# Two transformer blocks on one core: four staging tiles for weights, a new order of the opening, and GpSimd's long operations in pieces

## The chip, the cores and the metric

The kernel runs on one core of one Trainium2 chip. The metric is the device time of one execution in microseconds (us). The core has four compute engines that run beside each other: TensorE (PE in the profile; its weight loads are PEld), VectorE (DVE), ScalarE (ACT) and GpSimd (POOL). SyncE (SP) issues DMA transfers. Each engine takes its own instructions strictly in order, and engines wait for each other by semaphores.

## The reference

```python
x  = L0_attn_qkv                                     # (8, 256, 256)
xn = layernorm(x)
x  = x + attn0(xn) + ffn0(xn)                        # block 0
xn = layernorm(x)
x  = x + attn1(xn) + ffn1(xn)                        # block 1
```

`attn0` is causal attention with 16 heads of 16 channels and ALiBi slopes, with probabilities kept at or above 1e-10. `ffn0` has 8 experts, `silu(x @ Wg[e]) * (x @ Wu[e]) @ Wd[e]`, summed with weights that a small router makes from a sigmoid, a window and the two best. `attn1` is plain causal attention with its own weights. `ffn1` has two ternary layers: each weight becomes alpha * sign(W) where |W| is over 0.05 of the largest |W|, and alpha is the mean of those |W|; between them stands a gelu, and the result is quantized to 4 bits with one scale for the whole tensor.

## The kernel before, in words

The batch has 8 items of 256 tokens. The kernel makes one pass per item. Pass 0 (`"first"`) does block 0 of item 0 and the whole preparation of the weights; six passes of a loop (`"steady"`) and one more (`"last"`) do block 1 of one item beside block 0 of the next; `"final"` does block 1 of the last item and the quantization. So the list has nine parts, and only `"first"` loads and prepares weights.

The order of the work is written out by hand, as words in `ORDER_TEXT`, one text for each engine and kind of pass. A word names a step (`gate`, `score`, `split`) and its argument (`gate:2`: expert 2). Steps of one name run in the order of their arguments, whatever order the words have (`in_turn`). SyncE has no text of its own and follows TensorE's. An engine does for each word what its own `do` has under that name, or nothing.

The steps that matter here:

- `ln0a`, `ln0b`: layer norm of block 0 (VectorE; GpSimd makes `rstd` at L850). In pass 0 GpSimd then issues its own loads (`load_weights`, L818) and adds the bias `ob` (L844), and for that it waits for both `ob` loads.
- `split:i`: one of 14 weight tiles of 1024 columns, turned from float32 into a high and a low float16 part. SyncE loads it into a staging tile (`load_raw`, L674), ScalarE writes the high part (L965), and VectorE the low part (L1337). For splits 3, 5, 7, 9, 11 and 13 (`POOL_SPLITS`) ScalarE also writes a scaled copy (L967) and GpSimd makes the low part (L869). `SPLIT` lists them: 0 is the qk weights of block 0, 1, 3, 4, 6 ... are gate and up weights of experts 0, 1, 2, 3 ..., and 2, 5, 8, 11 are down weights of two experts each. There are two staging tiles, which borrow the room of `v_sb[1]` and `yx_sb`; the load of split i waits until the low part of split i - 2 is done.
- `vsplit`: the same for the v weights.
- `tr0`: transposes of the normed x (PE L1109), with high and low parts `xt_hi` (ACT L978) and `xt_lo` (DVE L1402). `xe` is GpSimd's copy of these for the experts (L875).
- `q0`, `k0` (PE L1135, ACT L995 and L998) and `l0` (DVE L1407): queries and keys with their parts. At `l0` SyncE stores them to DRAM (`store_parts`, L689) and reads them back in another layout (`load_stack`, L700).
- `v0`: values and the router's logits. `rt1`, `rt2`: the router.
- `setup:1` (GpSimd, L855 to L865): the four bias tables of the scores, from the slopes.
- `score` (PE L1223, DVE L1555, ACT L1037), `norm` (DVE L1580), `turn` (PE L1233, ACT L1046), `value`: attention of block 0.
- `gate`, `up`, `down`: an expert. At `up` VectorE writes `hid0` (L1502), ScalarE its high part `h_hi` (L1018) and GpSimd its low part `h_lo` (L880); `down` on TensorE (L1173) waits for that low part. `h1` is the same in block 1 (L903).
- `tern:i`, `tmx`, `tsm`: the two ternary weight matrices, 2048 columns each. VectorE finds the largest and the signs (L1345, L1352, L1355), GpSimd multiplies (L918), ScalarE sums (L958, L960), TensorE turns the sums (L1119), and VectorE makes alpha (L1370). TensorE starts the loop only when both are done.

GpSimd's text for pass 0 begins `ln0a xe split:3 setup:1 split:5 up`. The change does not touch it.

## Time and profile before

| | us |
|---|---|
| median of 3 runs | 765.38 (764.9 to 766.98) |
| profiled execution | 762.38 |
| its span, first to last instruction | 760.6 |

| engine | busy us | share |
|---|---|---|
| TensorE | 644.9 | 85% |
| VectorE | 570.8 | 75% |
| ScalarE | 465.4 | 61% |
| GpSimd | 270.1 | 36% |

The mean granted clock of TensorE was 0.958 of its full 2.4 GHz. All times below are us from the start of the span. A row of the timeline has its start, its duration, the engine, the line, the operation, output and inputs with their shapes (partitions x columns), a count, and in brackets how long the engine had been idle before it and what ended that. TensorE's matmuls overlap, so the distance between starts tells more than a duration. An engine with the letter q behind its name is the engine's instruction queue, which issues DMAs.

### The profile page before, as it was taken

The numbers are of one execution on the slowest core, as the hardware profiler recorded it, in microseconds if no ns is written. First come the engines' busy times: TensorE is split into PE (matmuls) and PEld (weight loads), VectorE is DVE, ScalarE is ACT, GpSimd is POOL, SyncE is SP. The second block draws the span as 40 slices with busy tenths as digits, with TensorE's granted clock in tenths as the row PEclk, the third lists the DMA queues.
The fourth block names the chain that finished last, engine by engine and source line by source line (L and its number), as shares of the span: only waits on it lengthen the run. The fifth ranks groups of instructions, "written<-read, shape, count | busy, mean of one in ns | idle before, by whom it ended". The sixth has DMA issues, their size and how long they took to land.

```text
span 760.6 us, 19948 instructions
## 1 busy us (share of the span) xinstructions
PE 644.9 (85%) x6455; PEld 480.6 (63%) x6455; DVE 570.8 (75%) x2203; ACT 465.4 (61%) x1223; POOL 270.1 (36%) x386
## 2 busy tenths in 40 slices
PE   1476676989989997999889997999899997999773
PEld 0354554767666775777666775777676775767542
DVE  4489867796687948796779858796779768886557
ACT  2567765954379454965389445965398435963652
POOL 7846541224404241142404241233313331135336
PEclk9989998999999999999999999999999998999996
DMA  6843021300303030302212030302211030300453
GB/s 203 273 127 117 8 77 49 97 17 16 124 14 110 14 110 28 109 1 69 83 35 76 14 110 28 110 4 68 80 58 53 14 110 16 112 3 1 153 181 110
DMA packets 49555, 56.72 MB, mean 75 GB/s; under 512 B 5104, under 2 KB 40048, under 8 KB 49520
## 3 DMA queue, kind: packets, MB, share of 16 engines
q1 hardware_dynamic: 46480, 52.44, 21.6%
q0 software_dynamic: 1056, 2.62, 1.0%
q10 hardware_dynamic: 1984, 1.21, 0.5%
q8 instruction: 19, 0.31, 0.2%
q14 instruction: 16, 0.13, 0.1%
HBM read 33.71 MB, written 22.54 MB: 74 GB/s over the span
## 4 chain that ended last, share of the span: by engine, by line
PE 58%; DVE 16%; ACT 11%; issue 8%; POOL 2%; DMA 2%; ACTq 1%; SPq 1%; DVEq 1%; POOLq 0%
PE gen_ps L1162 16%; PE gen_ps L1173 9%; PE gen_ps L1135 6%; PE value_ps L1280 5%; PE gen_ps L1193 4%; PE gen_ps L1210 3%; ACT hid L1025 3%; PE value_ps L1286 3%; PE score_ps L1223 2%; ACT probs L1037 2%; DVE probs L1555 2%; DVE inv L1591 2%; DVE probs L1580 2%; PE turn_ps L1249 2%; PE turn_ps L1233 2%
## 5 line engine op out<-in xcount | busy, mean ns | idle before, releaser
L880 POOL TENSOR_TENSOR h_lo<-hid,h_hi 128x512 f16<-128x512 f32 x64 | 74.4, 1163 | 271.6 <-ACT h_hi L1018 271.6
L1037 ACT ACTIVATE probs<-probs,nmax 128x256 f32<-128x256 f32 (+1 forms) x256 | 113.4, 446 | 29.0 <-DVE nmax L1555 28.6
L1162 PE MATMUL gen_ps<-xe_hi,gu_hi 128*128 128x256 f16 x512 | 101.0, 280 | 2.1 <-issue 2.1
L1162 PE MATMUL gen_ps<-xe_lo,gu_hi 128*128 128x256 f16 x512 | 100.6, 279 | 0.0
L1162 PE MATMUL gen_ps<-xe_hi,gu_lo 128*128 128x256 f16 x512 | 100.4, 279 | 0.0
L1555 DVE CUSTOM_DVE_ANT_0 probs<-score_ps,bias 128x256 f32<-128x256 f32 (+1 forms) x256 | 79.1, 351 | 16.5 <-PE score_ps L1225 16.5
L1065 ACT ACTIVATE et<-turn_ps 128x384 f32<-128x384 f32 x124 | 54.0, 489 | 50.9 <-PE turn_ps L1255 48.6
L1569 DVE CUSTOM_DVE_ANT_0 junk<-score_ps,bias 128x256 bf16<-128x256 f32 x248 | 73.6, 353 | 14.2 <-PE score_ps L1225 13.3
L1580 DVE TENSOR_SCALAR probs<-probs,rsum 128x256 f32<-128x256 f32 (+1 forms) x256 | 76.5, 341 | 4.6
L1014 ACT ACTIVATE tanh_sb<-gen_ps 128x512 f32<-128x512 f32 x64 | 37.8, 591 | 64.6 <-PE gen_ps L1162 64.5
L889 POOL TENSOR_SCALAR_AFFINE_SELECT et<-et 128x256 f32<-128x256 f32 x128 | 51.3, 423 | 73.0 <-ACT et L1065 73.0
L1223 PE MATMUL score_ps<-k_stack,q_stack 64*128 64x256 f16 x252 | 36.3, 285 | 44.0 <-DVE nmax L1555 26.0
L1046 ACT ACTIVATE pt<-turn_ps 128x384 f32<-128x384 f32 x128 | 60.4, 482 | 20.3 <-PE turn_ps L1235 20.2
L1173 PE MATMUL gen_ps<-wd_hi,h_hi 128*128 128x256 f16 x256 | 50.1, 278 | 9.7 <-issue 6.8
L1223 PEld LDWEIGHTS score_ps<-k_stack,q_stack 64*128 64x128 f16 x252 | 12.2, 93 | 72.2 <-DVE nmax L1555 30.7
L1162 PEld LDWEIGHTS gen_ps<-xe_hi,gu_hi 128*128 128x128 f16 x512 | 47.7, 100 | 14.3 <-issue 8.4
L1162 PEld LDWEIGHTS gen_ps<-xe_lo,gu_hi 128*128 128x128 f16 x512 | 51.3, 100 | 7.0
L1513 DVE SCALAR_TENSOR_TENSOR acc<-gen_ps,w,acc 128x256 f32<-128x256 f32 x112 | 48.8, 477 | 9.2 <-PE gen_ps L1173 9.2
L1162 PEld LDWEIGHTS gen_ps<-xe_hi,gu_lo 128*128 128x128 f16 x512 | 51.2, 100 | 6.9
L1502 DVE SCALAR_TENSOR_TENSOR hid<-gated,gen_ps 128x512 f32<-128x512 f32 x64 | 43.8, 684 | 11.4 <-PE gen_ps L1162 10.7
L903 POOL TENSOR_TENSOR h_parts<-hid,h_parts 128x512 f16<-128x512 f32 x32 | 37.3, 1178 | 38.4 <-ACT h_parts L1032 38.4
L1497 DVE SCALAR_TENSOR_TENSOR gated<-tanh_sb,gen_ps 128x512 f32<-128x512 f32 x64 | 43.6, 682 | 9.7 <-ACT tanh_sb L1014 9.7
(225 smaller groups left out, 1662.7 us busy)
## 6 DMA issues: line engine op xcount, KB each, us to landing
scr_q<-parts SPq DMA_DIRECT2D x32, 256.0 KB, 2.7
scr_k<-parts SPq DMA_DIRECT2D x32, 256.0 KB, 3.0
q_stack<-scr_q SPq DMA_DIRECT2D x64, 128.0 KB, 3.0
k_stack<-scr_k SPq DMA_DIRECT2D x64, 128.0 KB, 3.1
x<-in_x SPq DMA_DIRECT2D x8, 256.0 KB, 2.7
y_dram<-yx_sb SPq DMA_DIRECT2D x7, 256.0 KB, 2.2
x_dram<-yx_sb SPq DMA_DIRECT2D x7, 256.0 KB, 2.2
out_dram<-gu_hi SPq DMA_DIRECT2D x7, 256.0 KB, 2.2
```

The costliest lines, as they stand in the source:

```text
L880: pool.tensor_tensor(h0_lo[:, e], hid0[:, e], h0_hi[:, e], ALU.subtract).then_inc(s_h0l, 1)
L889: pool.affine_select(out=on_diagonal, in_=on_diagonal, compare_op=ALU.is_ge, fill=0.0, base=0, pattern=[[0, NT], [1, P]], channel_multipli ...
L1037: last = act.activation(probs[:, k, lo:hi], probs[:, k, lo:hi], ACT.Exp, scale=-1.0, bias=nmax[:, k, j:j + 1], accum_out=esum[:, k, j:j + 1])
L1046: act.activation(pt[:, slot:slot + 3].rearrange("p t q -> p (t q)"), turn_ps[s % 2][:, 0:3 * P], ACT.Copy).then_inc(s_ev[0], 1)
L1065: act.activation(et[:, s % TURNED], pair_of(st)[hp][:, 0:3 * P], ACT.Exp).then_inc(s_ev[1], 1)
L1162: last = pe.matmul(g[:, S * f:S * f + S], w[:, st.arg, m, k, cols], xx[:, k, :], start=(i == 0), stop=(i == len(terms) - 1))
L1173: last = pe.matmul(g[:, D * t:D * t + D], h[:, st.arg % 2, f, P * t:P * t + P], w[:, st.arg, f, :], start=(i == 0), stop=(i == len(terms) ...
L1223: pe.matmul(pair[hp][:, 0:S], q[rows[hp], i, P:S], k[rows[hp], i, :], start=True, stop=True)
L1513: dve.scalar_tensor_tensor(acc[:, t], g[:, D * t:D * t + D], w8[:, t, e:e + 1], (xb[0] if st.place == 0 else acc)[:, t], ALU.mult, ALU.add)\
L1555: last = dve.tensor_tensor_reduce(out=probs[:, k, lo:hi], in0=g[:, lo:hi], in1=bias0[:, s, blo:S], scale=-1.0, scalar=BIG, op0=ALU.add, op ...
L1569: last = dve.tensor_tensor_reduce(out=junk[:, hp, lo:hi], in0=pair_of(st)[hp][:, lo:hi], in1=bias1[:, blo:S], scale=-1.0, scalar=BIG, op0= ...
L1580: last = dve.tensor_scalar(probs[:, k, lo:hi], probs[:, k, lo:hi], rsum[:, k, j:j + 1], CLAMP, ALU.mult, ALU.max)
```

## The change

It has four parts.

1. Four staging tiles instead of two (`RAW = 4`). The new two take the room of the q and k stacks of block 1, which are now one tensor. The load of split i waits for the low part of split i - 4.
2. The small loads move. ScalarE issued fourteen loads ahead of its work; now it issues four (`bqk0`, `temp`, `vb0`, `wv0`), which have a semaphore of their own, `s_c0`. SyncE issues the others behind its first weight tiles. `setup:2` on VectorE needs only the first group; what belongs to block 1 is the new step `setup:3`.
3. A new order of pass 0's opening on TensorE, ScalarE and VectorE. `q0` and `k0` follow `tr0` at once, on TensorE and on ScalarE, and VectorE's `l0` comes ahead of `split:1`. VectorE's memset (`setup`) comes ahead of its wait for x. ScalarE's `split:1`, `split:2` and `split:3` stand behind `k0`.
4. GpSimd's long operations in pieces of 256 columns: the low part of a split in four, `h_lo` and `h1` in two, the ternary product in eight. The semaphore is raised by the last piece.

```diff
+RAW = 4
 "tensor": "first":
-            ln0a ln0b setup split xe split:1 setup:2 vsplit tr0 split:2 split:3 l0 q0 v0 split:5 k0 gate
-            setup:1 rt1 v0:1 norm:1 up gate:1 score norm split:4 rt2 score:1 up:1 split:6 down score:2
+            ln0a ln0b setup split xe split:1 setup:2 setup:3 vsplit tr0 q0 k0 l0 split:2 split:3 v0 split:5
+            gate setup:1 rt1 v0:1 norm:1 up gate:1 score norm split:4 rt2 score:1 up:1 split:6 down score:2
 "scalar": "first":
-            split:1 split vsplit tr0 split:2 q0 split:3 k0 gate v0 v0:1 split:5 split:4 gate:1 up score rt2
+            split tr0 vsplit q0 k0 split:1 split:2 split:3 gate v0 v0:1 split:5 split:4 gate:1 up score rt2
 "vector": "first":
-            ln0a split setup ln0b split:1 vsplit tr0 setup:2 split:2 v0 l0 gate rt1 v0:1 up split:4 gate:1
+            setup ln0a split ln0b setup:2 tr0 vsplit l0 split:1 v0 split:2 gate rt1 setup:3 v0:1 up split:4
+            gate:1 score score:1 up:1 norm rt2 norm:2 split:6 score:2 down gate:2 score:3 norm:1 score:4
...
+        stack1 = sb("stack1", [2 * KR, 2, 2, H // 4, S], F16)
+        q_stack.append([stack1[:, u, 0] for u in range(2)])
+        k_stack.append([stack1[:, u, 1] for u in range(2)])
...
+        raw += [stack1[:, u].rearrange("p a h n -> p (a h n)").bitcast(F32) for u in range(2)]
...
             def load_raw(i):
-                if i >= 2:
-                    sp.wait_ge(*lo_done(i - 2))
-                dst, (what, a) = raw[i % 2], SPLIT[i]
+                if i >= RAW:
+                    sp.wait_ge(*lo_done(i - RAW))
+                dst, (what, a) = raw[i % RAW], SPLIT[i]
...
-                if name == "split" and st.arg + 2 < len(SPLIT):
-                    load_raw(st.arg + 2)
+                if name == "split" and st.arg + RAW < len(SPLIT):
+                    load_raw(st.arg + RAW)
...
             load_x(Index(None, 0))
             load_raw(0)
             load_raw(1)
+            sp.dma_start(slope_sb[:], slopes.partition_broadcast(P)).then_inc(s_c, 16)
+            load_raw(2)
+            load_raw(3)
+            sp.dma_start(ob[0][:], ob0.partition_broadcast(P)).then_inc(s_ob, 16)
...
+            sp.dma_start(ob[1][:], ob1.partition_broadcast(P)).then_inc(s_ob, 16)
...
-                    pool.tensor_tensor(lo, raw[st.arg % 2], hi, ALU.subtract).then_inc(s_lop, 1)
+                    for c in range(0, 2 * NK * D, D):
+                        last = pool.tensor_tensor(lo[:, c:c + D], raw[st.arg % RAW][:, c:c + D], hi[:, c:c + D], ALU.subtract)
+                    last.then_inc(s_lop, 1)
...
-                    pool.tensor_tensor(h0_lo[:, e], hid0[:, e], h0_hi[:, e], ALU.subtract).then_inc(s_h0l, 1)
+                    for f in range(NF):
+                        last = pool.tensor_tensor(h0_lo[:, e, f], hid0[:, e, f], h0_hi[:, e, f], ALU.subtract)
+                    last.then_inc(s_h0l, 1)
...
-                        pool.tensor_tensor(tern_of(i)[0], tern_of(i)[0], tern_of(i)[1], ALU.mult).then_inc(s_tu, 1)
+                        w, t = tern_of(i)
+                        for c in range(0, NK * HID, D):
+                            last = pool.tensor_tensor(w[:, c:c + D], w[:, c:c + D], t[:, c:c + D], ALU.mult)
+                        last.then_inc(s_tu, 1)
...
         def _(act):
+            act.dma_start(bqk[0][:], bqk0).then_inc(s_c0, 16)
+            act.dma_start(half_t[:], temp.partition_broadcast(P)).then_inc(s_c0, 16)
+            act.dma_start(vb[0][:], vb0.partition_broadcast(P)).then_inc(s_c0, 16)
+            act.dma_start(wv_raw[0].rearrange("p (k n) -> p k n", k=NK), wv0.rearrange("(k p) n -> p k n", p=P)).then_inc(s_wv[0], 16)
```

## Rows read from the trace of the kernel before

**Rows 1.** The chain of waits in one steady pass, 375 to 460 us, by line.
```profile
by line: PE gen_ps L1162 17.2%; PE gen_ps L1173 9.7%; PE gen_ps L1135 8.3%; issue 6.9%; PE value_ps L1280 6.1%; PE gen_ps L1210 4.4%; PE gen_ps L1193 4.2%; ACT probs L1037 4.0%; ACT hid L1025 3.6%; PE value_ps L1286 3.1%; PE score_ps L1223 
```
**Rows 2.** Busy time by stretch: stretch, length, engines, clock, DMA; steady pass, then pass 0.
```profile
205.00:292.00 87.00, 80.98 (x824) 61.03 (x823) 66.52 (x273) 53.83 (x148) 25.80 (x41) 0.98 0.18 57
...
52.00:105.00 53.00, 39.48 (x345) 30.46 (x343) 48.88 (x139) 39.44 (x95) 23.20 (x22) 0.94 0.18 55
```
**Rows 3.** Timeline of the opening, all engines, 0 to 24 us.
```profile
1.31 0.46 SPq L679 DMA_DIRECT2D v_sb<-in_wqk  x1
...
10.73 1.06 ACT L965 ACTIVATE qk_hi<-v_sb 128x1024 f16<-128x1024 f32 x1
...
13.23 1.02 DVE L1317 MEMSET v_sb<- 128x1152 f32 x1 [0.19 <-issue]
...
20.32 0.84 ACT L995 ACTIVATE rest<-gen_ps,bqk 128x256 f32<-128x256 f32 x2 [0.53 <-PE gen_ps L1135]
...
21.29 0.38 PE L1135 MATMUL gen_ps<-xt_hi,qk_hi 128*128 128x256 f16 x2
...
21.73 1.04 ACT L965 ACTIVATE gu_hi<-yx_sb 128x1024 f16<-128x1024 f32 x1
...
22.67 1.04 ACT L967 ACTIVATE yx_sb<-yx_sb 128x1024 f32<-128x1024 f32 x1
...
23.79 2.12 POOL L869 TENSOR_TENSOR gu_lo<-yx_sb,gu_hi 128x1024 f16<-128x1024 f32 x1 [2.35 <-ACT yx_sb L967]
```
**Rows 4.** Timeline of GpSimd, 26 to 42 us.
```profile
26.41 2.75 POOL L861 TENSOR_TENSOR bias<-at,slope_sb 128x1024 f32<-128x1024 f32 x1
...
33.40 1.89 POOL L861 TENSOR_TENSOR bias<-at,slope_sb 128x1024 f32<-128x1024 f32 x1
...
38.69 2.13 POOL L869 TENSOR_TENSOR wd_lo<-yx_sb,wd_hi 128x1024 f16<-128x1024 f32 x1
40.77 1.15 POOL L880 TENSOR_TENSOR h_lo<-hid,h_hi 128x512 f16<-128x512 f32 x1
```
**Rows 5.** Timeline of TensorE: the first score and the first two `down` steps.
```profile
37.80 0.40 PE L1223 MATMUL score_ps<-k_stack,q_stack 64*128 64x256 f16 x2 [7.92 <-DMA k_stack<-scr_k]
...
42.02 0.38 PE L1173 MATMUL gen_ps<-wd_hi,h_hi 128*128 128x256 f16 x2 [1.05 <-issue]
...
48.89 0.58 PE L1173 MATMUL gen_ps<-wd_hi,h_hi 128*128 128x256 f16 x2 [3.34 <-issue]
```
**Rows 6.** Timeline of SyncE: the first store of q and k.
```profile
27.43 0.37 SPq L694 DMA_DIRECT2D scr_q<-parts  x1
```
**Rows 7.** Timeline: the two ternary products on GpSimd, and VectorE behind the first.
```profile
78.52 4.08 POOL L918 TENSOR_TENSOR hid<-hid,t_sb 128x2048 f32<-128x2048 f32 x1 [4.09 <-DVE t_sb L1355]
...
87.44 0.42 DVE L1370 TENSOR_REDUCE t_tot<-gen_ps 128x2 f32<-128x256 f32 x1 [1.34 <-PE gen_ps L1119]
...
104.79 5.10 POOL L918 TENSOR_TENSOR h_parts<-h_parts,t_sb 128x2048 f32<-128x2048 f32 x1 [8.98 <-DVE t_sb L1355]
```
**Rows 8.** DMA issues, 0 to 20 us: count, KB each, median us to landing.
```profile
v_sb<-in_wqk SPq DMA_DIRECT2D x1, 512.0 KB, 7.7
...
x<-in_x SPq DMA_DIRECT2D x1, 256.0 KB, 5.5
```
**Rows 9.** Chain of waits, 0 to 150 us: start, us; twelve matmuls at either clock.
```profile
17.50 2.73 PE gen_ps L1135 x12
...
93.17 1.31 PE gen_ps L1173 x12
```
**Rows 10.** Timeline of ScalarE: the high part of expert 1's `hid0`.
```profile
46.77 0.62 ACT L1018 ACTIVATE h_hi<-hid 128x512 f16<-128x512 f32 x1
```
**Rows 11.** Groups of GpSimd by shape: busy us, mean ns.
```profile
L844 POOL TENSOR_TENSOR xb<-acc,ob_sb 128x256 f32<-128x256 f32 x16 | 11.2, 723 | 39.8 <-DVE yx_sb L1543 36.8 <-DVEq L1617 2.9
```
**Rows 12.** Timeline, 146.5 to 149 us: VectorE beside GpSimd.
```profile
146.93 1.45 DVE L1580 TENSOR_SCALAR probs<-probs,rsum 128x256 f32<-128x256 f32 x2
...
147.10 1.20 POOL L903 TENSOR_TENSOR h_parts<-hid,h_parts 128x512 f16<-128x512 f32 x1 [2.94 <-ACT h_parts L1032]
```

More of the change, by code:

```diff
@@ L155 @@
         "first": """
-            ln0a split setup ln0b split:1 vsplit tr0 setup:2 split:2 v0 l0 gate rt1 v0:1 up split:4 gate:1
-            score score:1 up:1 norm rt2 norm:2 split:6 score:2 down gate:2 score:3 norm:1 score:4 down:1
-            norm:3 up:2 split:8 gate:3 score:5 norm:4 up:3 tern score:6 norm:5 tmx tern:1 gate:4 score:7
-            down:2 split:10 score:8 norm:6 norm:7 down:3 score:9 up:4 norm:8 score:11 score:10 norm:9
-            score:12 norm:11 tern:2 gate:5 down:4 score:13 +ln0a up:5 norm:10 norm:12 split:12 tsm tern:5
-            tern:6 score:14 gate:6 norm:13 up:6 +ln0b score:15 gate:7 down:5 tmx:1 norm:15 vsplit:1 norm:14
-            +tr0 up:7 down:6 tern:8 tern:7 +l0 +v0 +v0:1 op0 down:7 tsm:1 tern:11
+            setup ln0a split ln0b setup:2 tr0 vsplit l0 split:1 v0 split:2 gate rt1 setup:3 v0:1 up split:4
+            gate:1 score score:1 up:1 norm rt2 norm:2 split:6 score:2 down gate:2 score:3 norm:1 score:4
+            down:1 norm:3 up:2 split:8 gate:3 score:5 norm:4 up:3 tern score:6 norm:5 tmx tern:1 gate:4
+            score:7 down:2 split:10 score:8 norm:6 norm:7 down:3 score:9 up:4 norm:8 score:11 score:10
+            norm:9 score:12 norm:11 tern:2 gate:5 down:4 score:13 +ln0a up:5 norm:10 norm:12 split:12 tsm
+            tern:5 tern:6 score:14 gate:6 norm:13 up:6 +ln0b score:15 gate:7 down:5 tmx:1 norm:15 vsplit:1
+            norm:14 +tr0 up:7 down:6 tern:8 tern:7 +l0 +v0 +v0:1 op0 down:7 tsm:1 tern:11
         """,
@@ L501, in two_blocks @@
         s_x = sem("s_x")
+        s_c0 = sem("s_c0")
         s_c = sem("s_c")
@@ L508, in two_blocks @@
         s_w1 = sem("s_w1")
-        s_raw = [sem(f"s_raw{i}") for i in range(2)]
+        s_raw = [sem(f"s_raw{i}") for i in range(RAW)]
         s_scr = [sem(f"s_scr{l}") for l in range(2)]
@@ L902, in do @@
                     wait(pool, s_h1h, n.at(NH // 2, st.arg + 1))
-                    pool.tensor_tensor(h1_parts[:, 1, a:a + 2], hid1[:, a:a + 2], h1_parts[:, 0, a:a + 2],
-                                       ALU.subtract).then_inc(s_h1l, 1)
+                    for j in range(a, a + 2):
+                        last = pool.tensor_tensor(h1_parts[:, 1, j], hid1[:, j], h1_parts[:, 0, j], ALU.subtract)
+                    last.then_inc(s_h1l, 1)
                 if name == "quant":
@@ L962, in do @@
                     i = st.arg
-                    act.wait_ge(s_raw[i % 2], 16 * sum(2 if what == "gu" else 1 for what, _ in SPLIT[i % 2:i + 1:2]))
-                    act.activation(split_parts(i)[0], raw[i % 2], ACT.Copy, scale=WSCALE).then_inc(s_hi, 1)
+                    act.wait_ge(s_raw[i % RAW], 16 * sum(2 if what == "gu" else 1 for what, _ in SPLIT[i % RAW:i + 1:RAW]))
+                    act.activation(split_parts(i)[0], raw[i % RAW], ACT.Copy, scale=WSCALE).then_inc(s_hi, 1)
                     if i in POOL_SPLITS:
-                        act.activation(raw[i % 2], raw[i % 2], ACT.Copy, scale=WSCALE).then_inc(s_hi, 1)
+                        act.activation(raw[i % RAW], raw[i % RAW], ACT.Copy, scale=WSCALE).then_inc(s_hi, 1)
                 if name == "vsplit":
@@ L1078, in before_block1 @@
                 act.wait_ge(s_vlo, 2)
+                act.wait_ge(s_set, SET_ALL)
                 act.sem_inc(s_ev[1], H)
@@ L1152, in do @@
                     m = ("gate", "up").index(name)
-                    if st.arg == 0 and m == 0:
+                    if st.arg == 0:
                         wait(pe, s_xe, n.at(2, 2))
-                    if first and m == 0:
+                    if first:
                         pe.wait_ge(*lo_done(SPLIT.index(("gu", st.arg))))
@@ L1322, in do @@
                     dve.tensor_scalar(half_t[:], half_t[:], 0.5 / WSCALE, None, ALU.mult).then_inc(s_set, 1)
-                    dve.tensor_scalar(bqk[0][:, 0:2], bqk[0][:, 0:2], float(C) ** -0.5, None, ALU.mult)\
-                       .then_inc(s_set, 1)
-                    dve.tensor_scalar(bqk[1][:, 0:2], bqk[1][:, 0:2], float(C) ** -0.5, None, ALU.mult)\
-                       .then_inc(s_set, 1)
-                    for l in range(2):
-                        dve.tensor_scalar(vb[l][:], vb[l][:], WSCALE, None, ALU.mult).then_inc(s_set, 1)
+                    dve.tensor_scalar(bqk[0][:, 0:2], bqk[0][:, 0:2], float(C) ** -0.5, None, ALU.mult).then_inc(s_set, 1)
+                    dve.tensor_scalar(vb[0][:], vb[0][:], WSCALE, None, ALU.mult).then_inc(s_set, 1)
+                if name == "setup" and st.arg == 3:
+                    dve.wait_ge(s_c, 16 * NC)
+                    dve.tensor_scalar(bqk[1][:, 0:2], bqk[1][:, 0:2], float(C) ** -0.5, None, ALU.mult).then_inc(s_set, 1)
+                    dve.tensor_scalar(vb[1][:], vb[1][:], WSCALE, None, ALU.mult).then_inc(s_set, 1)
                 if name == "vsplit":
```

34 lines of the change are left out of this document (14 added, 20 removed).

## The prediction

> **What bounds the kernel now.** Read the steady passes first. In a pass of some 87 us TensorE is busy 81 us and VectorE 67 us, and the chain of waits of such a pass consists of TensorE, ScalarE and VectorE groups and holds none of GpSimd's [rows 1, 2]. Six of the nine passes look like that, so the edits to GpSimd's `h_lo` and `h1` steps can earn or cost little there. The first pass is different, and it is the only one whose loads and opening order change. It ends near 116 us, and two things bound it in turn.
>
> Up to 49 us it is GpSimd. ScalarE's scaled copy for split 3 ends at 23.71, and from 23.79 GpSimd runs without a pause: split 3, the four bias tables, split 5, the `h_lo` of expert 0, which ends at 41.92 [rows 3, 4]. TensorE had its first score at 37.80, did `up:1`, and then stood 1.05 us until the first `down` at 42.02: it came 0.1 us after that `h_lo`. The next `down` at 48.89 waits again (3.34 us) for an `h_lo` [rows 5]. The other branch of the opening is the round trip of q and k through DRAM: stored from 27.43, first score at 37.80 [rows 5, 6]. These two branches are nearly level at 42 us; that is the point of the whole case.
>
> From 52 to 105 us it is VectorE: busy 48.9 of 53 us, TensorE 39.5 [rows 2]. In this stretch stand two ternary weight tiles. For each, VectorE makes the signs, GpSimd multiplies 2048 columns (4.08 and 5.10 us), ScalarE sums, TensorE turns the sums, and VectorE waits for that: 1.34 us of idle before 87.44, and the second time the end of the pass hangs on it [rows 7].
>
> **The order of the opening and the four staging tiles.** Call T the time at which ScalarE begins the first split (10.73 before). Before, ScalarE had fourteen loads to issue first; its qk weights, issued at 1.31, had landed 7.7 later, at 9.0 [rows 3, 8]. After, ScalarE issues four loads, so T is the landing itself. With less traffic from ScalarE's queue in front it lands at 9.0 or sooner; 6.9 is my lower bound (x, which is in front of it on the queue, landed 5.5 after its issue [rows 8]). I take 8.0.
>
> From T to the first q matmul were 17.50 - 10.73 = 6.77 us [rows 3, 9], of which 1.02 + 0.19 were the memset that now stands before the wait for x: 5.6 remain. The ScalarE work on q starts 2.82 later (20.32) and takes 1.41 (to 21.73): T + 9.8. k follows q directly on TensorE: at the low clock at first and at the high one (which it had at 21.29) for the rest; twelve matmuls take 2.73 or 1.31 us at these levels, and the mix here about 1.8. So its ScalarE work begins at T + 10.3 and ends at T + 11.75, which is 19.75 [rows 3, 9]. VectorE then writes the low parts (1.2), and split 1 (1.2), on whose completion SyncE's load 5 waits ahead of the stores: stores at about 22.7 instead of 27.43, first score at 22.7 + 10.37 = 33.1 instead of 37.80 [rows 5, 6]. That is the gain of the new order: 4.7 us.
>
> But it is the gain of one branch. On ScalarE split 3 now stands behind k, split 1 and split 2. Four copies of 0.94 us (21.73 to 22.67) and the last one's end: T + 15.75 = 23.75, where it was 23.79 [rows 3]. **GpSimd's run starts no sooner.** Its parts: split 3 in four pieces 2.6 (below) for 2.1; the cast 0.5; four tables at (38.69 - 33.40)/2 = 2.65, that is 10.6, plus contention; split 5 in pieces 2.6; `h_lo` in two pieces 1.35. Contention: the first table took 2.75 beside 1.89 of an undisturbed one, because VectorE's low parts of q and k ran then; these are over by now, but VectorE's split 4 and the router's operations fall into the run, so I keep 0.8 (bounds 0 and 2.2). Sum 18.4 [rows 4]: `h_lo` 0 is done at 42.2 against 41.92. The low bound is 6.9 + 15.75 + 17.6 = 40.3, the high one 9.0 + 15.75 + 19.8 = 44.5.
>
> What the early score meets: TensorE does score and `up:1` until 36.2 and then has nothing until 42.3, six us instead of one. In the trace such a rest is followed by matmuls at the low clock: after 7.92 us (37.80) and after 3.34 us (48.89), where twelve matmuls take 2.73, while after the rest of 1.05 us at 42.02 they ran at the high one, where twelve take 1.31 [rows 5, 9]. So the first `down` costs 1.4 more, and the scores and transposes behind it about 0.4: `gate:2` (twelve more) ends 5.0 us after `h_lo` 0 instead of 3.6, by my count. ScalarE then gains: before, its step `up:1` came at 46.77 [rows 10] because splits 6 and 7 waited for loads that SyncE could not issue until the stacks were issued. With four tiles these are loaded when it wants them, and it takes tanh and `h_hi` at once: 0.1 + 0.5 + 0.6, GpSimd 1.35, TensorE at 5.0 + 2.75 = 7.8 us after `h_lo` 0; before 48.89 - 41.92 = 7.0. So the second `down` starts at 50.0 against 48.89: **+1.1 us** (bounds -0.8 and +3.5). VectorE, which before caught up only at 52, has slack now, but its list behind the score of head pair 4/5 is the same, and that score comes 2.7 us after this `down`. So the shift stays as it is until the ternary step.
>
> By the page "DMA: Bandwidth & Descriptors" of the Trainium skill (section "Issuing engines are not separate DMA queues") loads from all issuing engines share the same 16 DMA engines, so that another issuer saves only issue time. Were nothing gained in landing, T would be 9.0 and the sum 1.0 us higher; the range has that.
>
> **GpSimd's long operations in pieces.** 512 columns take 1.15 us, 1024 take 2.13, 2048 take 4.08 [rows 4, 7]: 1.9 ns for each column and near 0.2 for each instruction, of which some 0.05 lies beside its neighbour. 256 columns of float32 were measured at 0.72 in L844 [rows 11]; the line through the others gives 0.68. With 0.62 to 0.69 from piece to piece, a split of 1024 costs 2.6 (+0.5), `h_lo` 1.35 (+0.15 to 0.25), a ternary product 5.0 to 5.6 (+0.9 to +1.5). Splits 3 and 5 and the first `h_lo` are in the sum above. Both ternary products stand in the chain, each with someone idle behind it: **2 x 1.2 = +2.4 us**. Two further `h_lo` of the first pass add **+0.3**. In the steady passes the longer `h_lo` is hidden: it runs while TensorE is a gate and an up ahead; were that cover gone, it would be 8 x 0.2 in each of six passes, 10 us.
>
> In return VectorE waits less. At 146.93 two operations, 0.55 together in most places, took 1.45 while GpSimd's 512 columns ran from 147.10 [rows 12]. The page "SBUF — State Buffer" (section "Who interferes with whom") of the Trainium skill calls the pair of ports an exclusive lock, held for a whole instruction, whichever came first; the trace agrees. Pieces of 256 halve such a wait. I find some ten of them in the trace, of 0.5 to 1.4 us; about half would be given back and a third of that lies on the path: **-0.6 us** (bounds 0 and -2.5).
>
> **The rest** is taken at nothing: the thirteen loads that SyncE issues ahead of its list (about 0.5 us each, done near 10 us) stand before load 4, which waits for the first split anyway; ob1, now behind 3 MB, has no row for its new landing; it costs nothing as long as GpSimd's add and its copy for `xe`, some 3 us together, are over by 23.75, and moves split 3 if not.
>
> **The sum.** 1.1 + 2.4 + 0.3 - 0.6 = +3.2 us. The profiled execution took 762.38 (span 760.6), so 765.6 for one like it; it was 3 us under the median of the runs, 765.38, and on the median the forecast is 768.6. About 0.3% (2.3 us) is what a measurement of this kernel can tell from no change.
>
> **Rivals.**
> Rival 1, faster: the early score carries. It would if GpSimd's run were not what TensorE waits for at 42 us, for instance if split 3 began near 19 and `h_lo` 0 were done by 37.5. Then -4.7 + 2.7 - 0.6 = -2.6: 762.8. For it speaks that q and k really are in the chain before 38 us; against it that the 1.05 us of idle before 42.02 and the unbroken run of GpSimd are in the same trace. 2 in 10.
> Rival 2, no change: T at 6.9, no contention on the tables and pieces at 0.62: -0.8 + 1.8 + 0.2 - 1.0 = +0.2: 765.6. 2.5 in 10.
> Rival 3, clearly slower: the landing stays at 9.0 and the pieces meet VectorE's router operations, which take the ports between them. `h_lo` 0 comes at 44, and TensorE stands for 8 us. Decides when split 3 starts after 24.7: +3 + 3 + 0.4 = +6.4: 771.8. 1.5 in 10.
> The forecast itself, 4 in 10 (own range 767 to 770.5).
>
> Range: from under rival 1 to over rival 3, 762.0 to 773.0. Chances: slower 0.52, within 0.3% 0.27, faster 0.21.
>
> **What would show it.** First score near 33 us but the first `down` still near 42, with about 6 us of idle and a low clock behind it; GpSimd without a pause from 23.5 to 42; ternary products as eight pieces of 5.0 to 5.6 us in all; steady passes of unchanged length. It is wrong if `down:0` starts before 40, if the pieces come every 0.5 us, or if a steady pass changes by over 0.5 us.

## The result, and the profile after

| | before | after |
|---|---|---|
| median | 764.54 us (761.84 to 766.98, 20 runs) | 768.05 us (764.06 to 770.36, 20 runs) |
| profiled execution | 762.38 us | 764.06 us |
| its span | 760.6 us | 762.3 us |

The ratio is 1.0046, with a 95% interval from 1.0033 to 1.0058: the changed kernel is slower by 3.5 us. That is the "slower" of the forecast, and 0.5 us from its 768.6. Much of that nearness is luck, as the experiments show. The profiled execution of after is the fastest of its twenty, so one profile of each kernel says little about a total. Two profiles of the changed kernel end the first pass at 122.6 and 119.9 us (before: 117.6), a difference of 2.7 without any edit. So the ratios and medians carry the sums below, and a profile shows a place only where others of the same kind agree with it.

The page of the profile of after, its engines and its granted clock in 40 slices of 19 us:

```profile
PE 644.5 (85%) x6455; PEld 479.0 (63%) x6455; DVE 575.4 (75%) x2203; ACT 465.7 (61%) x1223; POOL 288.3 (38%) x514
PEclk9879798999999999999999999999999999999998
```

GpSimd is busy 288.3 us instead of 270.1: that is the bare price of the pieces, 18 us of work in all. TensorE, VectorE and ScalarE moved by 0.4, 4.6 and 0.3 us. In the largest group of the page the 64 `h_lo` of 1.16 us became 128 of 0.67.

The opening on ScalarE, and on SyncE the store and the reading back of q and k:

```profile
7.05 1.06 ACT L982 ACTIVATE qk_hi<-v_sb 128x1024 f16<-128x1024 f32 x1 [2.91 <-DMA v_sb<-in_wqk]
21.23 1.04 ACT L984 ACTIVATE stack<-stack 128x1024 f32<-128x1024 f32 x1
42.91 1.06 ACT L982 ACTIVATE gu_hi<-stack 128x1024 f16<-128x1024 f32 x1 [2.06 <-DMA stack<-in_wu]
...
20.90 0.37 SPq L692 DMA_DIRECT2D yx_sb<-in_wd  x1
21.31 0.51 SPq L700 DMA_DIRECT2D scr_q<-parts  x1
...
31.25 0.52 SPq L718 DMA_DIRECT2D q_stack<-scr_q  x1
...
36.29 0.59 SPq L690 DMA_DIRECT2D stack<-in_wg  x1
```

The qk weights landed 5.7 us after their issue, not 7.7 [rows 8], so T was 7.05 and not 8.0. The store of q left at 21.31 instead of 27.43 [rows 6]. But the reading back began 9.9 us behind it, where the trace of before has 5.3 (from 27.43 to 32.72). Of the 6.1 us that the new order gains on this branch, 4.6 are lost on the way through DRAM.

GpSimd from 19 to 42 us (answers to [rows 4]):

```profile
19.79 2.36 POOL L860 TENSOR_TENSOR xb<-x,ob_sb 128x256 f32<-128x256 f32 x2 [4.00 <-DMA ob_sb<-in_ob]
22.10 0.39 POOL L893 COPY xe_hi<-xt_hi 128x256 int32<-128x256 int32 x1
22.44 0.40 POOL L894 COPY xe_lo<-xt_lo 128x256 int32<-128x256 int32 x1
22.80 2.54 POOL L886 TENSOR_TENSOR gu_lo<-stack,gu_hi 128x256 f16<-128x256 f32 x4
25.31 0.39 POOL L872 CAST at<-at 128x256 f32<-128x256 int32 x1
25.84 1.89 POOL L877 TENSOR_TENSOR bias<-at,slope_sb 128x1024 f32<-128x1024 f32 x1
...
38.05 2.56 POOL L886 TENSOR_TENSOR wd_lo<-yx_sb,wd_hi 128x256 f16<-128x256 f32 x4
40.56 1.35 POOL L899 TENSOR_TENSOR h_lo<-hid,h_hi 128x256 f16<-128x256 f32 x2
```

The run of GpSimd begins at 22.80, 1.0 earlier than before, goes on without a pause and ends at 41.9, as before. Its first instruction waited for `ob`, which landed at 19.8. `xe` ended at 22.8, half a microsecond behind ScalarE's scaled copy (22.27), so the late `ob` held split 3 by 0.5.

TensorE where it stood still (answers to [rows 5]):

```profile
36.25 0.40 PE L1241 MATMUL score_ps<-k_stack,q_stack 64*128 64x256 f16 x2 [5.22 <-DMA k_stack<-scr_k]
42.01 0.38 PE L1191 MATMUL gen_ps<-wd_hi,h_hi 128*128 128x256 f16 x2 [2.58 <-issue]
49.73 0.59 PE L1191 MATMUL gen_ps<-wd_hi,h_hi 128*128 128x256 f16 x2 [2.63 <-issue]
```

The first `down` starts at the same 42.0 as before: the 1.5 us that the first score gained became idle time (2.58 instead of 1.05). The second came 0.8 later.

The ternary products (answers to [rows 7]):

```profile
81.19 5.09 POOL L941 TENSOR_TENSOR hid<-hid,t_sb 128x256 f32<-128x256 f32 x8 [4.80 <-DVE t_sb L1373]
108.80 6.10 POOL L941 TENSOR_TENSOR h_parts<-h_parts,t_sb 128x256 f32<-128x256 f32 x8 [8.84 <-DVE t_sb L1373]
```

5.09 and 6.10 us instead of 4.08 and 5.10, so 1.0 us more each. Steady passes, from one `rstd` of block 1 to the next, are 84.8 to 85.0 us each, and in before 84.6 to 84.7. In both kernels an occasional one takes 1.7 less. Two passes of after:

```profile
294.70:379.60 84.90, 78.72 (x806) 59.13 (x806) 65.37 (x269) 53.84 (x148) 27.41 (x52) 0.98 0.19 59
379.60:462.80 83.20, 77.05 (x806) 58.20 (x806) 65.31 (x269) 53.73 (x148) 27.35 (x52) 1.00 0.18 60
```

The columns are the stretch, its length, busy time and instructions of TensorE, its weight loads, VectorE, ScalarE and GpSimd, then clock, DMA share and GB/s. The two passes hold the same instructions. The mean clock of the pass isn't what decides: most short passes have 0.98 too. What decides is where the stretch of low clock (0.5, the lower of the two levels) lies. Here are three stretches of before. The first is in a pass of 84.7 us that began at 461.0, the others in one of 83.1 us that began at 545.7:

```profile
468.00:471.00 3.00, 3.00 (x18) 2.21 (x17) 2.96 (x21) 2.00 (x8) 0.50 (x1) 0.56 0.00 0
546.70:549.70 3.00, 2.90 (x16) 1.91 (x17) 2.93 (x15) 1.85 (x10) 0.00 (x0) 0.53 0.25 80
552.70:555.70 3.00, 3.00 (x30) 2.40 (x29) 2.96 (x21) 2.74 (x9) 0.50 (x1) 1.00 0.00 0
```

Near the start of each pass TensorE waits twice for VectorE, 0.59 and 1.37 us. In the short pass the low clock comes ahead of these waits, and only 0.57 us of them is left. In the long one it comes behind them, on matmuls without a gap, of which it does 18 in 3 us instead of 30. All 70 steady passes in the fourteen profiles of this case fit: in the 17 short ones the low clock lies 1 to 5 us into the pass or is missing, in the 53 long ones 6 to 11 us into it. The profile of before has two short passes and that of after one, so they differ by 1.7 us for no reason of the change.

### The profile page after: what moved, and what is told of

Same layout as the page of the kernel before. It is cut to its first block, busy times and chain, and to the rows that moved or that the text cites. A ratio compares the mean times of both kernels' runs of the same rounds, so it can differ in the third digit from the quotient of the medians.

```text
span 762.3 us, 20090 instructions
## 1 busy us (share of the span) xinstructions
PE 644.5 (85%) x6455; PEld 479.0 (63%) x6455; DVE 575.4 (75%) x2203; ACT 465.7 (61%) x1223; POOL 288.3 (38%) x514
## 4 chain that ended last, share of the span: by engine, by line
PE 58%; DVE 17%; ACT 11%; issue 8%; DMA 3%; POOL 1%; SPq 1%; DVEq 1%; ACTq 0%; POOLq 0%
PE gen_ps L1180 15%; PE gen_ps L1191 9%; PE gen_ps L1153 6%; PE value_ps L1298 5%; PE gen_ps L1211 4%; PE gen_ps L1228 3%; ACT hid L1042 3%; PE value_ps L1304 2%; ACT probs L1054 2%; PE score_ps L1241 2%; DVE probs L1573 2%; DVE inv L1609 2%; DVE probs L1598 2%; PE turn_ps L1251 2%; PE turn_ps L1267 2%
## 5 line engine op out<-in xcount | busy, mean ns | idle before, releaser
L899 POOL TENSOR_TENSOR h_lo<-hid,h_hi 128x256 f16<-128x256 f32 x128 | 83.6, 674 | 264.2 <-ACT h_hi L1035 264.2
L1598 DVE TENSOR_SCALAR probs<-probs,rsum 128x256 f32<-128x256 f32 (+1 forms) x256 | 78.2, 347 | 4.6
L924 POOL TENSOR_TENSOR h_parts<-hid,h_parts 128x256 f16<-128x256 f32 x64 | 41.9, 682 | 35.6 <-ACT h_parts L1049 35.6
L1035 ACT ACTIVATE h_hi<-hid 128x512 f16<-128x512 f32 x64 | 40.3, 630 | 21.3 <-DVE hid L1520 20.0
L1191 PE MATMUL gen_ps<-wd_hi,h_lo 128*128 128x256 f16 x256 | 50.1, 278 | 0.0
```

Of the source, the lines that this page charges most:

```text
L899: last = pool.tensor_tensor(h0_lo[:, e, f], hid0[:, e, f], h0_hi[:, e, f], ALU.subtract)
L1191: last = pe.matmul(g[:, D * t:D * t + D], h[:, st.arg % 2, f, P * t:P * t + P], w[:, st.arg, f, :], start=(i == 0), stop=(i == len(terms) ...
L1598: last = dve.tensor_scalar(probs[:, k, lo:hi], probs[:, k, lo:hi], rsum[:, k, j:j + 1], CLAMP, ALU.mult, ALU.max)
```

## The experiments

All ratios are to the kernel before, run on the same chip, whose median was 764.39 us in the first group, 764.14 in the second and 764.69 in the third. A cost in us is the ratio's, unless the text says that it is by the medians; the two can differ by 1 us. Every kernel computes everything.

### The opening alone, the pieces alone

`open_only` is the changed kernel with all GpSimd operations whole again:

```diff
-                    for c in range(0, 2 * NK * D, D):
-                        last = pool.tensor_tensor(lo[:, c:c + D], raw[st.arg % RAW][:, c:c + D], hi[:, c:c + D], ALU.subtract)
-                    last.then_inc(s_lop, 1)
+                    pool.tensor_tensor(lo, raw[st.arg % RAW], hi, ALU.subtract).then_inc(s_lop, 1)
```

and so on for `h_lo`, `h1` and the ternary product.

> The changed kernel with all of GpSimd's operations whole again, so that four staging tiles, the moved loads and the new order are left. My theory (the early score waits for GpSimd's run of split 3, tables, split 5 and h_lo; the pieces cost 1.0 us on each ternary product): split 3 starts at 22.8, h_lo 0 ends near 41, the first down starts near 41 and the second near 49; pass 0 ends 1 to 3 us later than before, because the low clock behind the long rest stays, and without the 2 us of the ternary pieces; 764.5 to 767 against 764.5. Rival A (the new order is what costs, the pieces are neutral): as slow as the full change, 768. Rival B (the order gains 4 us and the pieces eat it): 760 to 761.

Measured: 762.32 us, ratio 0.9973 [0.9952, 0.9994]. The opening alone (tiles, moved loads and new order together, which no run takes apart) makes the kernel faster, by 2.1 us. Expected was no gain (764.5 to 767).

`pieces_only` is the other half: the kernel before with the four operations in pieces.

> The kernel before with only GpSimd's operations in pieces. My theory: each ternary product 5.1 us instead of 4.1, the run to the first h_lo 1.1 us longer (43.0), the first down at 43; pass 0 ends 3 us later; the waits of VectorE's norm step on GpSimd in the first pass of the loop shrink from 3 us in all to under 1. Sum +1 to +3: 765.5 to 767.5. Rival A: no change, 764.5. Rival B: +4 to +5, 769.

Measured: 768.04 us, ratio 1.0061 [1.0037, 1.0085], 4.7 us slower (3.7 by the medians), more than the theory's +1 to +3. So the whole loss is in the pieces. How much the opening takes back when the pieces are there isn't clear of noise: the changed kernel measured 1.0046 here and 1.0066 in a second measurement.

### Which pieces

`after_whole_tern`: the changed kernel with the ternary product as one instruction. `h_pieces_only`: the kernel before with `h_lo` and `h1` in two pieces each. `tern_pieces_only` and `split_pieces_only`: the kernel before with one of the other edits, for instance

```diff
-                        pool.tensor_tensor(tern_of(i)[0], tern_of(i)[0], tern_of(i)[1], ALU.mult).then_inc(s_tu, 1)
+                        w, t = tern_of(i)
+                        for c in range(0, NK * HID, D):
+                            last = pool.tensor_tensor(w[:, c:c + D], w[:, c:c + D], t[:, c:c + D], ALU.mult)
+                        last.then_inc(s_tu, 1)
```

> The changed kernel with the two ternary products whole, all else as changed. My theory: the products take 4.1 and 5.1 us instead of 5.1 and 6.1, TensorE's turn of the sums comes 1.0 and 2.0 us sooner, pass 0 ends 2.0 us sooner than in the changed kernel: 766. If the products were hidden: unchanged at 768. If VectorE's waits on the whole products came back in the path: 767 to 768.

> The kernel before with only h_lo and h1 in two pieces (splits and ternary products whole). My theory: pass 0 longer by 0.3 to 0.6 (three h_lo in its chain), the norm steps of VectorE in the first pass of the loop shorter by up to 2 us on the path: -1.5 to 0, that is 763 to 764.5. Rival (longer h_lo and h1 cost in every pass): 8 times 0.15 in each pass, some +5: 769.

> The changed kernel once more, beside the others of this call: 768, 3 to 4 us over before. Its profile shows which marks repeat: split 3 at 22.8, first score at 36, h_lo 0 at 41.9, the ternary products at 81 and 109, the first pass of the loop from 122.6. If the opening's marks differ by over 0.5 us from the first profile, they can't carry a term of that size.

> The kernel before with only the two ternary products in eight pieces. My theory: each 5.1 us for 4.1, both on the chain, +2.0 to +2.4 in pass 0: 766.5 to 767. Rival (the 3.2 us that whole products gave in the changed kernel came from TensorE's clock at the start of the loop and not from the products): +1, 765.5.

> The kernel before with only the six low parts on GpSimd in four pieces each. My theory: 0.45 for each of splits 3 and 5 in the run to the first h_lo (42.4 to 42.8) and 0.45 for split 7 in front of an h_lo near 60; +0.5 to +1.4: 765 to 766. Rival (the splits are hidden): 764.4.

| | median us | ratio, 95% |
|---|---|---|
| after_whole_tern | 764.85 | 0.9999 [0.9978, 1.0021] |
| h_pieces_only | 763.68 | 0.9991 [0.9972, 1.0011] |
| after_again (the changed kernel) | 768.61 | 1.0066 [1.0048, 1.0084] |
| tern_pieces_only | 767.02 | 1.0029 [1.0012, 1.0046] |
| split_pieces_only | 766.98 | 1.0035 [1.0016, 1.0055] |

The ternary pieces cost 2.2 us alone in before (2.9 by the medians), and 3.6 as the last edit of after (1.0046 less 0.9999; 5.1 with the 1.0066 of `after_again`); the forecast had 2.4. The pieces of the splits cost 2.7, and the forecast had 1.0; the expectation's 765 to 766 was too low. Those of `h_lo` and `h1` together cost nothing or earn a little.

Where the 1.7 us too little for the splits lie, the trace of `split_pieces_only` shows. TensorE's stops, then ScalarE and GpSimd near 60 us:

```profile
42.84 0.59 PE L1175 MATMUL gen_ps<-wd_hi,h_hi 128*128 128x256 f16 x2 [2.14 <-issue]
51.56 0.38 PE L1175 MATMUL gen_ps<-wd_hi,h_hi 128*128 128x256 f16 x2 [2.49 <-issue]
...
62.21 0.62 ACT L1020 ACTIVATE h_hi<-hid 128x512 f16<-128x512 f32 x1
...
61.08 2.56 POOL L870 TENSOR_TENSOR gu_lo<-yx_sb,gu_hi 128x256 f16<-128x256 f32 x4 [0.73 <-ACT yx_sb L969]
63.59 1.17 POOL L882 TENSOR_TENSOR h_lo<-hid,h_hi 128x512 f16<-128x512 f32 x1
```

The first `down` moved by 0.8, as the two splits in front of it say. But the second `down` moved by 2.7 [rows 5], and the granted clock from 42 to 50 us was 0.59, where before has 0.91: TensorE had stood for 2.14 us instead of 1.05. Later splits stand ahead of an `h_lo` as well: the one at 61.08 holds an `h_lo` whose `h_hi` ended at 62.83. The forecast counted splits 3 and 5 only and took those behind 49 us as free.

### Which branch holds the first `down`

`tables_first_whole` is meant to take GpSimd's branch out of the way. It has the changed opening and the bias tables ahead of `split:3`, while the loads of `wo` and of the ternary weights go behind (`h1` stays in two pieces, the rest is whole):

```diff
                     if early:
-                        load_weights()
+                        bias_tables()
                         pool.wait_ge(s_ob, 32)
                         add_bias()
```

> The changed opening, with GpSimd's four bias tables moved from behind split 3 to right behind rstd, its ternary loads behind split 3 and its wo loads behind the first two h_lo; splits, h_lo and ternary products whole, h1 in two pieces. If GpSimd's run is what the early score waits for, h_lo 0 is done by 34 to 36 and the first down follows score and up:1 with no rest: first down near 36 to 39 instead of 42, at the high clock, the second down near 44 to 46, pass 0 ends 3 us or more sooner than with the tables behind split 3: 757 to 761. If another wait (the load of split 6 or 7, ScalarE, VectorE's router) takes its place, the second down stays at 48 to 49: 762.

Measured: 763.1 us, ratio 0.9994 [0.9971, 1.0017]. Here are GpSimd's `h_lo` 0, TensorE's first score and second `down`, and the two splits on ScalarE between them:

```profile
35.15 2.12 POOL L902 TENSOR_TENSOR h_lo<-hid,h_hi 128x512 f16<-128x512 f32 x1
...
38.65 0.40 PE L1242 MATMUL score_ps<-k_stack,q_stack 64*128 64x256 f16 x2 [5.12 <-DMA k_stack<-scr_k]
51.97 0.58 PE L1192 MATMUL gen_ps<-wd_hi,h_hi 128*128 128x256 f16 x2 [6.14 <-issue]
...
43.37 1.06 ACT L983 ACTIVATE gu_hi<-stack 128x1024 f16<-128x1024 f32 x1 [1.43 <-DMA stack<-in_wu]
47.63 1.06 ACT L983 ACTIVATE gu_hi<-stack 128x1024 f16<-128x1024 f32 x1 [3.21 <-DMA stack<-in_wu]
```

`h_lo` 0 was done at 37.3, 4.6 us sooner than in before, and the first `down` started at 41.6 all the same: the score came at 38.65 and `up:1` behind it ended there. But that score was 2.4 us later than in after (36.25). The ternary loads, moved as well, now lay beside the reading back of q and k, which took 8.2 to 8.5 us from issue to landing instead of 3.1. So the run shows that the `down` follows the score once `h_lo` 0 is early. It does not show what an early `h_lo` is worth with the score where it was. The fair comparison is `open_h1_pieces` below (0.9912), the same kernel without these moves: together they cost 0.0082 of the time, 6 us (5 by the medians). A third thing then stands in the way: ScalarE takes splits 6 and 7 ahead of its step for expert 1, and both waited for their loads. SyncE issues them behind the eight loads of the stacks. The second `down` came at 52.0, 3 us later than before.

`late_ternary_loads` asks what delayed the stores of q and k. It is the changed kernel with GpSimd issuing the two 1 MB loads of the ternary weights behind split 3.

```diff
                     last.then_inc(s_lop, 1)
+                    if st.arg == 3:
+                        load_ternary()
```

> The changed kernel with the two loads of the ternary weights (1 MB each) issued by GpSimd behind split 3 instead of at 14.1 and 14.9 us. It computes everything. 'Loads in the way': the stores of q and k, which landed 8.35 us after their issue beside these loads and 3.8 us in the kernel before, land in 4 to 5 us, and the first score moves from 36.2 to about 32.5; ob lands earlier and split 3 starts at 22.3. GpSimd's h_lo 0 still ends at 41.5 to 42 and the time stays within 1 us of the changed kernel: 767.5. 'Loads not in the way' (the split weights that SyncE itself loads are what the stores stand behind): the stores still take 8 us and the first score stays at 36: 768.1. If instead the early score alone were worth what the kernel with the opening gained, the time would fall to 765 with h_lo 0 unchanged.

Measured: 768.67 us, ratio 1.0065 [1.0041, 1.0089]. SyncE's loads back, TensorE's first score, and GpSimd:

```profile
21.82 0.51 SPq L700 DMA_DIRECT2D scr_q<-parts  x1
28.01 0.52 SPq L718 DMA_DIRECT2D q_stack<-scr_q  x1
...
37.02 0.40 PE L1246 MATMUL score_ps<-k_stack,q_stack 64*128 64x256 f16 x2 [6.21 <-DMA k_stack<-scr_k]
...
25.80 0.74 POOL L843 DMA_DIRECT2D hid<-in_w1t  x1
26.54 0.93 POOL L845 DMA_DIRECT2D h_parts<-in_w2t  x1
27.47 1.38 POOL L875 CAST at<-at 128x256 f32<-128x256 int32 x1
```

The stores now landed in 4.3 and 4.4 us (median from issue to landing; 7.4 for q and 7.9 for k in after), and the loads back left at 28.0 instead of 31.25. So the ternary loads were what delayed the stores. But moved, they delayed the loads back just as much: 6.9 us from issue to landing, where after has 3.1. The first score came at 37.0, 0.8 later than in after and not near 32.5 as expected. The issues and the slower cast put 2.7 us into GpSimd's run, and the first `down` came at 44.45. The ratio stands beside 1.0046 and 1.0066 for the changed kernel in its two measurements, although that `down` was 2.4 us late. Whether such a shift is taken up later isn't shown: VectorE's search of the largest began at 60.2, and at 59.5 and 57.4 in two profiles of after, so these two differ by nearly as much as the shift.

### The best combination

From the first groups a better kernel follows: the new opening with only the helpful pieces. `open_h_pieces` is `open_only` with `h_lo` and `h1` in two pieces, `open_h1_pieces` is `open_only` with `h1` alone in two pieces:

```diff
-                    pool.tensor_tensor(h1_parts[:, 1, a:a + 2], hid1[:, a:a + 2], h1_parts[:, 0, a:a + 2],
-                                       ALU.subtract).then_inc(s_h1l, 1)
+                    for j in range(a, a + 2):
+                        last = pool.tensor_tensor(h1_parts[:, 1, j], hid1[:, j], h1_parts[:, 0, j], ALU.subtract)
+                    last.then_inc(s_h1l, 1)
```

`open_h1_late` adds the late ternary loads to that.

> The changed kernel with its splits and ternary products whole, and only h_lo and h1 in pieces of 256 columns. It computes everything. Two theories. 'Relief': the pieces of h1 shorten the waits of VectorE's norm pairs in the first loop pass (1.45, 1.45 and 1.94 us in the kernel with the opening alone), and the pass that took 88.8 us there takes about 85.5, as in the kernel before with these pieces alone (85.4); h_lo 0 and the first pass cost 0.5 us of that: 762.3 - 3.3 + 0.5 = 759.5 us, with VectorE's three norm pairs at 0.96, 0.55 and 0.61. 'Same pool': the opening and the relief earn the same slack, because the first loop pass ends with the same tail of TensorE work: 762.0, no better than the opening alone.

> As the kernel before it in this call, but with h_lo whole too, so only h1 in pieces. It computes everything. If the relief comes from h1, as the place of the shortened norm pairs (beside GpSimd's h1 step) says, this one keeps all of it and pays nothing in the first pass: 0.3 to 0.6 us below the run with both in pieces, 759 us. If it comes from h_lo, the first loop pass is back at 88.8 us and the norm pairs at 1.45: 762.3.

> The best parts together: the opening of the changed kernel, h1 alone in pieces, and the ternary loads behind split 3. It computes everything. If the late loads leave the first down where it was (41.0 in the kernel with the opening alone), the time is that of the kernel with the opening and h1 in pieces, 759 us. If the first norm and up steps gain from an earlier score, 758. If the ternary weights land too late for VectorE's search of the largest (near 58 us), or the weights of splits 8 to 13 are delayed, 761 or more.

| | median us | ratio, 95% |
|---|---|---|
| open_h_pieces | 760.28 | 0.9952 [0.9922, 0.9982] |
| open_h1_pieces | 757.98 | 0.9912 [0.9881, 0.9943] |
| open_h1_late | 761.39 | 0.9956 [0.9929, 0.9983] |

`open_h1_pieces` is the fastest: 6.7 us under the kernel before, 10 under the changed one. Its gain over `open_only` is 0.0061 of the time, 4.7 us (about 3 either way; 4.3 by the medians). It lies where "relief" put it, in the first loop pass. First `open_only`, then `open_h1_pieces`, VectorE's scaling of the probabilities beside GpSimd's `h1`:

```profile
145.51 1.45 DVE L1590 TENSOR_SCALAR probs<-probs,rsum 128x256 f32<-128x256 f32 x2
150.04 1.46 DVE L1590 TENSOR_SCALAR probs<-probs,rsum 128x256 f32<-128x256 f32 x2
152.39 1.93 DVE L1590 TENSOR_SCALAR probs<-probs,rsum 128x256 f32<-128x256 f32 x2
145.68 1.21 POOL L919 TENSOR_TENSOR h_parts<-hid,h_parts 128x512 f16<-128x512 f32 x1 [2.95 <-ACT h_parts L1041]
```

```profile
144.54 0.96 DVE L1591 TENSOR_SCALAR probs<-probs,rsum 128x256 f32<-128x256 f32 x2
148.58 0.55 DVE L1591 TENSOR_SCALAR probs<-probs,rsum 128x256 f32<-128x256 f32 x2
150.13 0.62 DVE L1591 TENSOR_SCALAR probs<-probs,rsum 128x256 f32<-128x256 f32 x2
144.71 1.35 POOL L920 TENSOR_TENSOR h_parts<-hid,h_parts 128x256 f16<-128x256 f32 x2 [2.95 <-ACT h_parts L1042]
```

The three pairs take 2.13 us instead of 4.84. The first loop pass takes 85.1 us instead of 88.8. The 1.0 us beyond the pairs fits TensorE's clock. Behind the third pair, 35 to 45 us into the pass, in `open_only` and in `open_h1_pieces`:

```profile
153.57:163.57 10.00, 8.08 (x68) 5.67 (x69) 8.54 (x41) 5.79 (x21) 1.83 (x2) 0.83 0.01 2
152.25:162.25 10.00, 9.98 (x100) 7.51 (x99) 9.79 (x53) 7.31 (x25) 2.35 (x3) 1.00 0.01 2
```

In the first TensorE stood 3.12 us for VectorE and then ran at the low clock; in the second there is neither. The steady passes are unchanged within 0.2 us: in `open_only` from 295 to 385 us none of these pairs takes over 0.56, so there is nothing to relieve.

`h_lo` in pieces on top of that costs 3.1 us by the ratios and 2.3 by the medians, for which the forecast had 0.5. Both ratios have a half-width of 0.003, so the cost is not separated from zero by this pair alone. Where it lies in the first pass isn't shown. That pass ends at 119.4 instead of 117.2, but in `open_only`, with the opening of `open_h1_pieces`, it ends at 118.6. One part is plain: in the seven profiles with `h_lo` in pieces a long steady pass takes 84.8 to 85.0 us (one took 84.5), in the seven with it whole 84.6 to 84.8. Five such passes, one of them short, add up to some 422.8 us against 421.8, so about 1 us.

The late loads cost 3.4 us here, just clear of noise, and nothing clear of it in the changed kernel. The expectation's third case (761 or more) holds, but its reason isn't shown: the first score came at 39.7, the first `down` at 43.4, and the first pass ended 5.7 us later than in `open_h1_pieces`. Why the two kernels differ in this stays open.

**Where the time lies, by pass.** From one profile of each kernel (two of the changed one), in us:

| | end of the first pass | first loop pass |
|---|---|---|
| before; `tern_pieces_only` | 117.6; 120.7 | 91.1; 91.2 |
| `open_only`; `split_pieces_only` | 118.6; 123.8 | 88.8; 88.9 |
| the changed kernel, twice | 122.6; 119.9 | 87.2; 87.3 |
| `pieces_only`; `late_ternary_loads` | 123.6; 123.7 | 87.3; 87.3 |
| `h_pieces_only`; `after_whole_tern` | 119.3; 121.9 | 85.4; 84.9 |
| `open_h_pieces`; `open_h1_pieces` | 119.4; 117.3 | 85.2; 85.1 |
| `open_h1_late`; `tables_first_whole` | 122.9; 124.7 | 84.3; 84.4 |

In the first two rows `h1` is whole, in the others it is in pieces. Two things set the length of the first loop pass, and they add. `h1` in pieces takes 3.4 to 4.0 us off it. The other 2 us are the way it begins. The first 20 us of the pass in before and in `open_only`:

```profile
117.62:137.62 20.00, 16.24 (x127) 12.18 (x125) 15.53 (x78) 13.30 (x44) 1.86 (x2) 0.85 0.05 13
118.57:138.57 20.00, 17.89 (x144) 13.97 (x142) 17.83 (x84) 15.52 (x47) 1.86 (x2) 0.83 0.04 14
```

The clock is low for about as long in both. In before TensorE waits 1.37 us for VectorE near 126 us and meets a second stretch of low clock behind it; in `open_only` 0.33 of that wait is left and the low clock is over by then. It is the same difference as between long and short steady passes. Rows 1, 3 and 4 begin in the first way, the others in the second. So what `open_only` gains over before lies here in the profiles (88.8 instead of 91.1), and not in the first pass, which ended 1.0 later. With the ternary product whole the changed kernel gains 2.3 us here, and in the first pass 0.8 or -2.0, by which profile of it one takes. Alone in before the same pieces cost 3.1 us in the first pass and nothing here. What makes a kernel begin the loop in one way or the other isn't shown.

## Why the prediction was right, and where only by offset

**The bound.** Right: at 42 us GpSimd's branch holds the first `down`, with the other close behind. With after's score 1.5 us sooner `down:0` kept its place. With `tables_first_whole`'s `h_lo` 4.6 us sooner it moved by 0.4 only, but there the score was later too. "GpSimd's run starts no sooner" is wrong by 1.0: it started at 22.80, and 0.5 of what T gained was lost to `ob`. The sum of the run was 18.4 by forecast and 19.1 by the trace, with contention on two of the four tables (1.43 instead of 0.65 in their second half, twice). `h_lo` 0: forecast 42.2, measured 41.9.

**The early score.** The forecast had 33.1. T and the store were sooner than it said (7.05 and 21.31, against 8.0 and 22.7). What failed is the step "22.7 + 10.37": it took the round trip through DRAM over from [rows 5, 6], although the stores now run beside the ternary loads. The round trip was 14.9 us. So TensorE stood for 2.6 us and not for six, and of the low clock behind the rest one of two profiles of after shows something: 0.76 from 42 to 50 us, and 1.00 in the other, where before has 0.91. The place of the first `down` didn't change by it, because GpSimd's branch held it anyway.

**"With four tiles these are loaded when it wants them"** was wrong. ScalarE waited 2.06 us at 42.91 for split 6 and 0.47 for split 7, in before 1.38 and 0.86. The number of tiles wasn't the limit: SyncE's list is in order, and the loads of splits 6 and 7 stand in it behind the stacks, at 36.29 here and at 37.74 in before. `down:1` came at 49.7 and, in a second profile, at 48.8: +0.8 and -0.1 for a forecast of +1.1, with wrong parts in it.

**The terms of the sum, by the ratios:**

| edit | forecast | measured |
|---|---|---|
| opening, without its share of pieces (1.1 - 1.2) | -0.1 | -2.1 (-3.7 to -0.5) |
| splits in pieces (inside the opening's term) | +1.0 | +2.7 (1.2 to 4.2) |
| ternary products in pieces | +2.4 | +2.2 (0.9 to 3.5) in before, +3.6 in after |
| `h_lo` in pieces (0.2 in the opening, 0.3 behind) | +0.5 | +3.1 (-0.2 to 6.4), not separated from 0 |
| relief by pieces, `h1` | -0.6 | -4.7 (about ±3) |
| all | +3.2 | +3.5 |

The ternary step was right in size: 1.0 us per product by the trace. Its place holds for before, whose first pass became 3.1 us longer. In the changed kernel its larger cost lies in how the loop begins, which the prediction didn't have; the rival in the expectation of `tern_pieces_only`, TensorE's clock at the start of the loop, is true of that part. Two terms were too high for the kernel (the opening and the relief, by 2 and 4 us) and two too low (the splits and `h_lo`, by 1.7 and 2.6); so the total was met by offset. Measured one by one the terms add up to 1.2 us (2.6 with the ternary products as in after), the whole to 3.5. The difference lies within the intervals of the terms. "In the steady passes the longer `h_lo` is hidden" put at nothing what the profiles show as 0.1 to 0.2 us a pass, about 1 us in all.

The relief is the largest miss, and outside its own bounds (0 and -2.5). In the changed kernel itself the first loop pass is 3.8 us shorter than in before. The prediction said "about half would be given back and a third of that lies on the path" of some ten waits over the whole span. The three that count lie within 8 us of one pass, of their 3.2 us of waiting 2.7 were given back, and there VectorE was what the pass waited for. [rows 12] showed one of them, and the length of that pass, 91.1 us against 84.7 for its neighbours, was there to be read. As an estimate from these numbers, the first pass and the rest must then have cost some 6 us (3.5 + 3.8 - 1), where the forecast had 3.8; the two profiles of after show 5.0 and 2.3 in the first pass.

The page "SBUF — State Buffer" of the Trainium skill (section "Who interferes with whom") has the lock held for a whole instruction. The pairs above agree: with `h1` whole, 0.55 becomes 1.45 to 1.93, and with half the instruction, 0.55 to 0.96.

**What the prediction called wrong:** "if `down:0` starts before 40" (it started at 42.0), "if the pieces come every 0.5 us" (0.64), "if a steady pass changes by over 0.5 us" (0.2). None of the three came. Of the signs for it, the score near 33 and the rest of six us didn't come either.

**The rivals.** The first, "the early score carries", needed `h_lo` 0 by 37.5. `tables_first_whole` had such an `h_lo` but not the early score, which came at 38.65, and got 763.1. In no run did the first score come before 36.2, so this rival was never tested. The second, no change, had T at 6.9 and pieces at 0.62; they came at 7.05 and 0.64, close to it, and the kernel was slower all the same, by costs that neither it nor the forecast had. The third needed split 3 after 24.7; it started at 22.80.

What isn't settled: how the opening alone gains 2.1 us. The first `down` came 1.0 sooner in `open_only` than in before, but in `open_h1_pieces`, with the same opening, it came at 41.9, so that mark doesn't repeat. What both have is the shorter beginning of the loop. Nor is it known which of the opening's three parts earns it. Loads of splits 6 and 7 ahead of the stacks, which the traces point to as the next step, weren't tried.

## What to carry to other kernels

In this kernel cutting a long instruction of a helper engine in pieces was worth it only where its partner waited for the shared ports within a stretch that the partner bounds. Look for such stretches in a pass that is longer than its neighbours, and cut there alone. Everywhere else each cut costs its fixed part, and where someone waits for the last piece that cost is on the path.

Before a difference of 1 or 2 us between two profiles is explained, compare passes that hold the same instructions. Here they differ by 1.7 us by the place at which the clock is low.

When an order is changed to send a transfer sooner, price its flight by the traffic that it will meet, not by its old row, and look at what stands behind it on the same in-order queue: more buffers don't help a load that can't be issued.
